# Masked cross-attention tiles of a four-block transformer kernel: scores, masks and maxima on 32x32 parts of the array, masks copied into four partition groups and loaded for each tile

## The reference

```python
energy = jnp.einsum('nqhd,nkhd->nhqk', q, k)          # q 512, k 1601, h 16, d 16
energy = jnp.where(mask == 0, jnp.float32(-1e+20), energy)
attn = jax.nn.softmax(energy / math.sqrt(EMBED), axis=3)
out = jnp.einsum('nhql,nlhd->nqhd', attn, v).reshape(N, q_len, HEADS * HEAD_DIM)
return out @ w_out.T + b_out
```

## Time and profile before

| | |
|---|---|
| median of 3 executions | 3416.82 us (3416.21 to 3418.89) |
| profiled execution | 3416.62 us |
| its span, first to last instruction | 3414.8 us |
| mean granted clock of TensorE | 0.978 of full |
| TensorE (PE) busy | 3261.6 us, 96% |
| VectorE (DVE) busy | 1981.4 us, 58% |
| ScalarE (ACT) busy | 1437.7 us, 42% |
| blocks 3 and 4 | about 2041 to 3411 us of the span |

### The profile page before, as it was taken

The page is one execution under the profiler, slowest core; times in us unless marked ns, Lnnn a source line. Parts: engine busy times, 40 slices in busy tenths (PEclk is TensorE's granted clock), DMA queues, the critical chain, the costliest instruction groups (busy, mean ns, idle before and its releaser), DMA issues.

```text
span 3414.8 us, 45075 instructions
## 1 busy us (share of the span) xinstructions
PE 3261.6 (96%) x18319; PEld 1406.2 (41%) x18335; DVE 1981.4 (58%) x4290; ACT 1437.7 (42%) x1645; POOL 954.6 (28%) x469
## 2 busy tenths in 40 slices
PE   7999999999999999999987979899999999999999
PEld 3444444444434444444433852223333333333344
DVE  4444456554655546655574038776777676766446
ACT  3433344445434454344433213454444444545533
POOL 4655555654465444646300001010000000000000
PEclk9999999999999999999988999999999999999999
DMA  3000000000000000000031511111001111000000
GB/s 151 12 13 13 28 13 13 7 12 32 7 21 12 13 28 12 21 12 7 4 113 51 156 56 23 47 55 36 16 27 33 42 31 33 27 27 16 13 19 19
DMA packets 44601, 108.31 MB, mean 32 GB/s; under 512 B 4833, under 2 KB 23913, under 8 KB 43882
## 3 DMA queue, kind: packets, MB, share of 16 engines
q1 hardware_dynamic: 39018, 90.48, 8.0%
q0 software_dynamic: 5376, 14.95, 1.9%
HBM read 95.20 MB, written 16.78 MB: 33 GB/s over the span
## 4 chain that ended last, share of the span: by engine, by line
PE 85%; DVE 6%; ACT 4%; POOL 3%; issue 1%; DMA 1%; SPq 0%; ACTq 0%; POOLq 0%; DVEq 0%
PE ring L1267 11%; PE pv L1161 10%; PE ring L1150 9%; PE pv L1289 9%; PE ring L1228 3%; PE ring L1260 3%; PE ring L1131 3%; PE ring L1122 3%; PE ring L1108 3%; PE ring L1123 3%; PE ring L1147 3%; PE ring L1109 2%; PE ring L1273 2%; ACT wide L1436 2%; PE ring L1346 2%; PE ring L1327 2%
## 5 line engine op out<-in xcount | busy, mean ns | idle before, releaser
L1533 POOL TENSOR_TENSOR wide<-wide 124x1024 f32<-124x1024 f32 (+1 forms) x341 | 803.5, 2356 | 178.7 <-ACT wide L1429 140.8
L1436 ACT ACTIVATE wide<-ring 124x1024 f32<-124x1024 f32 (+2 forms) x544 | 528.1, 1022 | 532.4 <-PE ring L1267 530.1
L1652 DVE TENSOR_REDUCE max_a<-ring 128x2 f32<-128x802 f32 x512 | 493.7, 991 | 395.7 <-PE ring L1131 395.3
L1429 ACT ACTIVATE wide<-ring 124x1024 f32<-124x1024 f32 (+1 forms) x416 | 425.3, 1027 | 438.1 <-PE ring L1150 384.5
L1680 DVE CUSTOM_DVE_ANT_0 rest<-ring,slim 128x401 bf16<-128x401 f32 x683 | 374.9, 576 | 120.7 <-PE ring L1228 114.9
L1150 PE MATMUL ring<-wide 64*124 64x512 f32 (+1 forms) x1664 | 424.7, 588 | 0.0
L1161 PE MATMUL pv<-wide 124*64 124x512 f32 (+1 forms) x1664 | 411.8, 610 | 8.2 <-ACT wide L1429 8.2
L1690 DVE TENSOR_REDUCE slim<-ring 128x2 f32<-128x1024 f32 x256 | 308.1, 1222 | 112.4 <-PE ring L1240 110.9
L1267 PE MATMUL ring<-slim 32*128 32x512 f32 x2176 | 353.3, 648 | 3.0 <-ACT wide L1436 2.7
L1503 POOL DMA_DIRECT2D slim<-in_ctx_k x16 | 8.9, 560 | 985.6 <-PE ring L1228 937.0
L1530 POOL TENSOR_TENSOR wide<-wide 124x1024 f32<-124x1024 f32 x31 | 73.0, 2356 | 599.3 <-ACT wide L1429 586.0
(11 more groups left out here) (241 smaller groups left out, 4060.1 us busy)
## 6 DMA issues: line engine op xcount, KB each, us to landing
slim<-in_ctx_k SPq DMA_DIRECT2D x16, 800.5 KB, 4.4
wide<-in_w_pair SPq DMA_DIRECT2D x32, 384.0 KB, 3.1
wide<-in_w SPq DMA_DIRECT2D x16, 512.0 KB, 4.9
wide<-in_we SPq DMA_DIRECT2D x16, 512.0 KB, 3.9
slim<-in_ctx_v SPq DMA_DIRECT2D x16, 428.2 KB
wide<-in_ctxT SPq DMA_DIRECT2D x4, 1601.0 KB, 6.6
slim<-in_ctx_k POOLq DMA_DIRECT2D x16, 400.2 KB, 4.7
wide<-padded_x SPq DMA_DIRECT2D x8, 640.0 KB, 4.9
```

The source lines that it names most:

```text
L1429: sc.activation(exps_a[0:kn, slot_of[unit], :], slot[0:kn, :], ACT.Exp, scale=WIDE ** -0.5).then_inc(scalar_done, 1)
L1436: sc.activation((exps_2 if blk == 2 else exps_34)[0:kn, first + 2 * i:first + 2 * i + 2, :].rearrange("p h n -> p (h n)"), ring_t[0:kn, ba ...
L1533: po.tensor_tensor(sums[0:kn, :], sums[0:kn, :], view, ALU.add).then_inc(pool_done, 1)
L1652: ve.reduce_max(max_a[:, :, q, c], slot.rearrange("p (h n) -> p h n", h=2)[:, :, 0:CHUNK], AX.X).then_inc(vector_done, 1)
```

## The change

1. `scoreb` of block 3: key tiles are 128 wide (`MASKED_TILES`; the last has 65). Each head's product is cut into four matmuls of 32 columns of weights, so each goes to its own 32x32 part of the array. The mask is added in the same way: for each head and each strip of 32 keys a 32x32 identity times a 32 x 512 mask strip, ahead of the scores, for heads 0 and 1 and then for heads 2 and 3. A tile has 16 mask matmuls and 16 float32 ones where it had 4 and 4.
2. The 32 rows of a row part can only read their own 32 partitions, so each mask tile must lie in all four partition groups. `store_mask` writes the masks once to DRAM; `load_mask` loads a tile's strips four times, by four DMAs on SP, into one of four places (`MASK_PLACES`), for each of the 208 tiles anew. The load for tile n + 4 waits until the scores of tile n are done.
3. `max3`: 8 matmuls with 32 columns of weights in place of 2. `maxb` and `scoreb` of block 4 are cut likewise (8 for 2, 16 for 4). Block 2 stays.
4. `mask_keys` is two VectorE instructions on 128 partitions in place of three; SBUF places move; values are padded to 128 rows for each tile.
5. The costs in `Step` change (`scoreb` of block 3 from 2.0 to 1.1, block 4 from 0.88 to 0.95), so slots and warming matmuls may fall elsewhere. `TURNS_1` and `TURNS_3` stay.

```diff
+MASKED_TILES = [(k, min(P, CTX - k)) for k in range(0, CTX, P)]
+MASK_PLACES = 4
...
+    if k == "load_mask":
+        return f"{k}{unit[1] % MASK_PLACES}", GROUP
...
-                                   (4, 4 if b or g else 1))
+                                   (16, 16 if b or g else 1))
...
-        masks = (2.0, (1, 1), 1.5, 0.55) if blk == 3 else (0.88, (4, 4), 0.88, 0.0)
+        masks = (1.1, (16, 16), 1.1, 0.0) if blk == 3 else (0.95, (16, 16), 0.95, 0.0) if blk == 4 else (0.88, (4, 4), 0.88, 0.0)
...
+            if blk == 3:
+                n = (b * GROUPS + g) * NKT + k + MASK_PLACES
+                if n < B * GROUPS * NKT:
+                    emit(on(("load_mask", n), ("tensor", unit)))
...
     def masks_fill(slim_done):
         for s in range(2):
-            k3_free[s] = v3_free[s] = slim_done
+            k3_free[s] = v3_free[s] = slim_done + (("dma", ("store_mask",)),)
         free["xnT3"] = slim_done
+        emit(on(("store_mask",), ("vector", ("mask_keys",))))
+        for n in range(MASK_PLACES):
+            emit(on(("load_mask", n), ("dma", ("store_mask",))))
...
+                elif kind == "store_mask":
+                    for j in range(GROUP):
+                        sp.dma_start(masks[:, :, j, :].rearrange("k i n -> i k n"), maskT_sb[j * PAD:(j + 1) * PAD, :, :]).then_inc(done_sem, 16)
+                elif kind == "load_mask":
+                    n, = a
+                    for h in range(GROUP):
+                        sp.dma_start(mask_places[n % MASK_PLACES][h * PAD:(h + 1) * PAD, :, :], masks[n % NKT]).then_inc(done_sem, 16)
...
-                    for i in range(2):
+                    for i, j in product(range(2), range(P // PAD)):
                         own = slice(PAD * (2 * hp + i), PAD * (2 * hp + i + 1))
-                        last = pe.matmul(slot[:, i * BANK:i * BANK + CHUNK], queries_low(3, g)[own, q * P:(q + 1) * P],
+                        last = pe.matmul(slot[j * PAD:(j + 1) * PAD, i * BANK:i * BANK + CHUNK],
+                                         queries_low(3, g)[own, q * P + j * PAD:q * P + (j + 1) * PAD],
                                          keys_low(3, g)[own, CTX_CHUNKS[c]:CTX_CHUNKS[c] + CHUNK], start=True, stop=True)
...
-                        past.wait_ge(*at("vector", "mask_keys"))
-                        for h in range(2):
-                            pe.matmul(head_bank(unit, h), ident_b[0:kn, :], maskT_sb[0:kn, k, :],
-                                      start=True, stop=False)
-                    for h in range(GROUP):
-                        own = slice(PAD * h, PAD * h + PAD)
-                        if h == 2:
+                        n = (b * GROUPS + g) * NKT + k
+                        past.wait_ge(*at("dma", "load_mask", n))
+                    for first in (0, 2):
+                        if first:
                             for lane, other in plan.second_free[unit]:
                                 past.wait_ge(*at(lane, *other))
-                        last = pe.matmul(head_bank(unit, h), key_columns(blk, g, k0)[own, :],
-                                         queries_place(blk, g)[own, :], start=blk != 3 or h >= 2, stop=blk != 3 or h < 2)
-                        if h == 1:
-                            last.then_inc(tensor_done, 1)
-                    if blk == 3:
-                        for h in range(2, GROUP):
-                            last = pe.matmul(head_bank(unit, h), ident_b[0:kn, :], maskT_sb[0:kn, k, :],
-                                             start=False, stop=True)
-                    last.then_inc(tensor_done, 1)
+                        if blk == 3:
+                            for h, (c0, cn) in product(range(first, first + 2), parts):
+                                own = slice(PAD * h, PAD * h + cn)
+                                pe.matmul(head_bank(unit, h)[c0:c0 + cn, :], ident_b[own, own],
+                                          mask_places[n % MASK_PLACES][own, c0 // PAD, :], start=True, stop=False)
+                        for h, (c0, cn) in product(range(first, first + 2), parts):
+                            own = slice(PAD * h, PAD * h + PAD)
+                            last = pe.matmul(head_bank(unit, h)[c0:c0 + cn, :], key_columns(blk, g, k0)[own, c0:c0 + cn],
+                                             queries_place(blk, g)[own, :], start=blk != 3, stop=True)
+                        last.then_inc(tensor_done, 1)
```

57 lines of the change are left out of this document (30 added, 27 removed).

## The result

| | before | after |
|---|---|---|
| median | 3416.82 us | 3398.36 us (3396.06 to 3401.42, 5 executions) |
| profiled execution's span | 3414.8 us | 3396.6 us |
| mean granted clock | 0.978 | 0.971 |

The ratio is 0.9943, 95% interval 0.9932 to 0.9954: 18 us faster, where 91 were forecast. The time lies in the wide range (3250 to 3420) and outside the likeliest case's own (3255 to 3390).

A forecast was written before the change was run, and what follows sets the result against it. TensorE was taken to bound blocks 3 and 4, with about a third of rounds closed by ScalarE's ring slots. Tile -108, block 4 scores +2, clock +12, expert stage +3 gave -91: 3326 us, 8-in-10 range 3250 to 3420.

The forecast's parts named there:

- likeliest case: Whole kernel: the summed forecast of 3326 us with its bounds, 3255 to 3390, given a chance of 0.68.
- The failed step: Block 3's masked tile: sixteen 32x32 parts run side by side, so a tile takes 1.32 us against 2.16.
- The 0.84 of a tile: Block 3's masked tile: TensorE time saved per tile, 175 us over 208 tiles if nothing else binds.
- Rival 3: Block 3's tile halves take turns, heads 2 and 3 starting late: tile 2.44 us, +77, 3494 us; chance 0.12.
- Dense rounds: Block 3 rounds where the chain leaves TensorE after the first half: 0.35 us less each, 25 us over 70 rounds.
- the lower bound of 0.35: Masked tiles: least saving per tile, if the ring binds at once; 73 us over 208 tiles.
- Ring: Slots ScalarE must empty: 70 rounds go through ScalarE and save only 0.35 us each; the other 138 save 0.60.
- Maxima at 0: Block 3's maxima, 512 units: further starts cost 20 us, fewer mode changes save up to 20, so they cancel.
- Clock, 12 us: TensorE waits for slots more often, lowering the granted clock: 12 us added, bounds 0 and about 50.
- Mask loads hidden: Block 3's mask loads: there 5.6 to 10 us after a place is free, about 14.5 us available, so cost 0.
- Expert stage, 3 us: Mask store and first mask loads ahead of an expert-row load: a stall of 0 to 17 us, taken as 3.
- rival 2: TensorE's instruction feed binds at 25 ns a pair: tile 1.8 us, no change overall, about 3413 us; chance 0.09.

The follow-up runs named there:

- masks_outside: Changed kernel, only a tile's order differs: masks then scores of heads 0 and 1, second-slot wait, scores then masks of heads 2 and 3; 3364.35 us, ratio 0.9848.
- tile_wide: Changed kernel with block 3's tile as before (full-array masks, 128-column scores), maxima and block 4 scores still small; 3427.72 us, ratio 1.0029 to before.
- half_exp_before: Kernel before with block 3's ScalarE exponentials halved, 512 columns in place of 1024; ratio 0.9955 to before.

## Why the prediction was wrong, point by point

- **The failed step: "I take it that rows and columns combine: masks 0.24, two passes 0.98 ... Sum 1.32."** They do combine when the products stand in the right order (1.35 for the 16 scores alone, 1.57 from first start to last end with all masks first). In the order of the change they take 2.34, where the kernel before takes 2.16. The nearest rows had at most eight passes in the list; a tile now has 48, and how many waiting ones TensorE looks past was not in the sum. The 0.84 of a tile that finds its slots free was -0.18. The order is the cause: masks_outside changes nothing else, at the same clock, and gains 34 us.
- **Rival 3 had the mechanism** ("it looks past at most the 16 instructions of four heads. A half now is 48"), with a tile of 2.44 against 2.34 measured, and a chance of 0.12. Its sign was wrong, because it took the second exponential of a dense round to come on the path. Dense rounds got shorter (the lower quarter from 3.98 to 3.69), and two tiles that follow each other overlap (3.74 for two against 4.32). The point from which it decides, 2.16, was passed, and the kernel was still faster.
- **Dense rounds**: 0.35 less for the first half forecast; in the median of the tiles the exponential begins 0.33 earlier (1.44 for 1.77). Right. Over 208 tiles the chain gives 46 us from tile and 12 from exponentials, 0.28 for each, below the lower bound of 0.35 that the sum had.
- **Ring**: named, but too small. 70 rounds through ScalarE were counted from the chain; a wait for the second slot costs 0.74 in the mean of all 208, clock included, and in 141 of them the second half starts over 0.3 us behind the first. A chain shows who came last, not who came nearly last.
- **Maxima at 0**: the sum holds (8.2% of the chain before and after), the argument with "they cancel" only half: 10 us worse beside a wide tile, 65 better beside a small one, of which about half goes with the clock.
- **Clock, 12 us**: 0.97 to 0.92 over the 400 us from 2041 on, 20 us; later the same 0.99. Right in sign and roughly in size. tile_wide keeps 0.97 there, so it comes with the tile on small parts; how is not shown. In other versions it is the largest term that nobody forecast (0.87 with the wait ahead, 0.83 with wide maxima, 0.77 with wide scores).
- **Mask loads hidden**: right, 2.7 us from issue to landing and 0.9937 against 0.9943 without them. Not foreseen: 3 us at a gather.
- **Expert stage, 3 us**: it cost nothing. The changed kernel is 1.8 us late at 1974 us, but 2.1 late already at 1445, ahead of the first mask transfer (1919.79), and so is half_exp_before, which has no such transfers.
- **Instruction feed (rival 2)**: excluded. 16 mask products start within 54 ns, float32 ones 7 ns apart. The floor of 25 ns that the Trainium skill gives ("TensorE: Matmul & The Clock Gate", section "Wait — 56ns, not 53.3ns?") does not hold between different parts. Its sum also left out the other terms (17 us) that rival 3 counts.
- **Step costs**: not priced in the prediction; at most some 6 us in favour.

## What to carry to other kernels

Products on many small parts of the array run side by side only if few others wait ahead of them: put the independent ones first in the list and those that accumulate onto them afterwards, and count passes (a float32 product has two) for each part and in all. Keep neighbours in the list on the same cut of the array, since a change drains it. And before a shorter tile is turned into time, ask which slot it needs first: here an order that saved 0.58 us a tile lost 0.74 by asking for its second slot early. Compare the clocks of two versions by stage before a difference is put down to anything else.

## What the runs showed of the hardware that was not expected

- TensorE looks past three waiting passes of one 32x32 part, not four; and past 18 in all on 6 parts, not 24 on 8.
- Products on different parts start 3 to 4 ns apart in bfloat16 (16 of them within 54 ns), 7 in float32. Those that come after a stand of the list start 17 ns apart, as in the loose tile of the change.
- A 32x32 tile with wide scores takes 2.93 us, with small ones 1.63 in the best order: the drains, with the overlap that they prevent, cost 1.3.
- A busy TensorE can be at the lower clock: small masks with wide scores brought it down (above), and so did a single part. Here are two windows of the products by themselves (length; PE and PEld busy; DVE and POOL busy; clock, DMA share, GB/s): one product after another on a single part, and 32x32 products on all 16 parts. In the first it is busy 93.50 of 94 us at 0.50, the level of 1.2 GHz, in the second at 1.00.

```profile
406.00:500.00 94.00, 93.50 (x126) 17.29 (x127) 0.00 (x0) 0.00 (x0) 0.50 0.00 0
...
250.00:258.00 8.00, 7.88 (x184) 3.64 (x162) 0.00 (x0) 0.00 (x0) 1.00 0.01 2
```
